# A four-layer graph network on one core: who makes the low halves in the first layer, the order of its stores and loads, and how early the first normalised tiles are made

## The reference

```python
h = jnp.maximum(_layernorm(x, axis=-1), 0.0)
x = x + _L0_gnn_ref(h, adj, L0_gnn_weightr, L0_gnn_weightd, L0_gnn_bias)
h = jnp.maximum(_layernorm(x, axis=-1), 0.0)
x = x + _L1_gnn_ref(h, adj, L1_gnn_W1, L1_gnn_W2)
h = jnp.maximum(_layernorm(x, axis=-1), 0.0)
x = x + _L2_gnn_ref(h, adj, L2_gnn_W, L2_gnn_b)
h = jnp.maximum(_layernorm(x, axis=-1), 0.0)
x = x + _L3_gnn_ref(h, adj, L3_gnn_W, L3_gnn_a, L3_gnn_wtrans)
return x
```

## Time and profile before

| | us |
|---|---|
| median of 3 runs (2110.57 to 2112.67) | 2111.86 |
| the profiled execution, own time | 2112.05 |
| its span in the trace | 2110.3 |
| PE busy | 2052.6 (97%) |
| DVE busy | 1326.5 (63%) |
| ACT busy | 1012.9 (48%) |
| POOL busy | 53.6 (3%) |

### The profile page before, as it was taken

The page is one execution under the profiler, slowest core; times in us unless marked ns, Lnnn a source line. Parts: engine busy times, 40 slices in busy tenths (PEclk is TensorE's granted clock), DMA queues, the critical chain, the costliest instruction groups (busy, mean ns, idle before and its releaser), DMA issues.

```text
span 2110.3 us, 26133 instructions
## 1 busy us (share of the span) xinstructions
PE 2052.6 (97%) x10560; PEld 1493.7 (71%) x10560; DVE 1326.5 (63%) x2040; ACT 1012.9 (48%) x1333; POOL 53.6 (3%) x88
## 2 busy tenths in 40 slices
PE   5999989999999999999999899999999999999998
PEld 4888865555545555554555588888888888888887
DVE  6855440000044242434548899999999999999674
ACT  6755440000020000001104679797888788787873
POOL 0011340000000000000000000000000000000000
PEclk9999999999999999999999999999999999999999
DMA  9997352010311223301157645444445444351200
GB/s 376 381 349 278 111 202 48 21 41 21 100 50 56 65 64 96 117 31 61 48 109 313 170 160 207 138 180 145 180 144 179 165 140 180 132 212 65 100 20 11
DMA packets 102393, 288.25 MB, mean 137 GB/s; under 512 B 45184, under 2 KB 52096, under 8 KB 85760
## 3 DMA queue, kind: packets, MB, share of 16 engines
q1 hardware_dynamic: 96896, 278.19, 38.3%
q10 hardware_dynamic: 5376, 8.39, 1.3%
HBM read 245.11 MB, written 33.06 MB: 132 GB/s over the span
## 4 chain that ended last, share of the span: by engine, by line
PE 90%; DVE 3%; DMA 2%; ACT 2%; POOL 1%; issue 1%; SPq 0%; ACTq 0%; POOLq 0%; DVEq 0%
PE ps L1822 41%; PE ps L1733 32%; PE ps L1593 7%; PE ps L1750 7%; PE ps L1792 2%; DMA h_spill<-work 1%; POOL work L649 1%; PE ps L1699 1%; DMA feat<-in_adj 1%; PE ps L1671 1%; PE ps L1660 1%; ACT big L686 0%; DMA big<-in_adj_t 0%; POOL work L664 0%; DVE feat L1426 0%
## 5 line engine op out<-in xcount | busy, mean ns | idle before, releaser
L1733 PE MATMUL ps<-big,feat 128*128 128x512 fp8e4 x3072 | 671.1, 381 | 11.3 <-DMA feat<-h_spill 7.1
L1733 PEld LDWEIGHTS ps<-big,feat 128*128 128x128 f16 x3072 | 301.4, 98 | 375.0 <-issue 12.9
L1822 PE MATMUL ps<-big,work 128*128 128x257 f32 x2048 | 450.9, 381 | 4.9 <-ACT work L961 4.9
L1822 PE MATMUL ps<-big 128*128 128x257 f32 x2048 | 449.4, 380 | 3.5 <-ACT big L961 3.5
L1822 PEld LDWEIGHTS ps<-big,work 128*128 128x128 f32 x2048 | 388.4, 190 | 60.8 <-issue 4.8
L1822 PEld LDWEIGHTS ps<-big 128*128 128x128 f32 x2048 | 388.3, 190 | 59.6 <-ACT big L961 4.4
L1593 PE MATMUL ps<-feat,big 128*128 128x256 f16 x2048 | 224.7, 273 | 0.0
L1593 PEld LDWEIGHTS ps<-feat,big 128*128 128x128 fp8e4 x2048 | 199.9, 98 | 23.4
L686 ACT ACTIVATE big<-big 128x2048 bf16<-128x2048 f32 (+1 forms) x124 | 182.3, 1487 | 13.2 <-DMA big<-in_adj_t 12.9
L953 ACT ACTIVATE big<-feat,uv_sb 128x512 f32<-128x512 f32 x256 | 163.3, 710 | 22.5 <-PE ps L1822 22.5
L953 ACT ACTIVATE work<-feat,uv_sb 128x512 f32<-128x512 f32 x256 | 163.4, 713 | 16.5 <-PE ps L1822 15.8
(11 more groups left out here) (165 smaller groups left out, 1365.9 us busy)
## 6 DMA issues: line engine op xcount, KB each, us to landing
big<-in_adj_t SPq DMA_DIRECT2D x64, 1024.0 KB, 4.9
feat<-in_adj SPq DMA_DIRECT2D x56, 1024.0 KB, 6.9
big<-in_adj_t SPq DMA_DIRECT2D x80, 512.0 KB, 9.6
h_spill<-work SPq DMA_DIRECT2D x31, 512.0 KB, 3.6
feat<-h_spill SPq DMA_DIRECT2D x31, 512.0 KB, 4.7
work<-in_adj_t SPq DMA_DIRECT2D x27, 512.0 KB, 6.7
x_spill<-work SPq DMA_DIRECT2D x24, 512.0 KB, 2.7
feat<-in_adj_t SPq DMA_DIRECT2D x21, 512.0 KB, 8.6
```

The costliest lines, as they stand in the source:

```text
L1733: ins = mm(ps[:, bank + f, :], parts[:, j, h, f * P:(f + 1) * P], adj_units[:, c, j, :], start=(fresh and h == 0), stop=(end and h == 1), ...
L1822: ins = mm(ps[:, 4 * s + t, 0:YW], quads[k % RING][:, jj, t * P:(t + 1) * P], Yb[:, j, s, :], start=(j == 0), stop=(j == NT - 1), skip_gro ...
```

## The change

`FIRST_TILE` goes from 2 to 0 and `STATS_AHEAD` from 4 to 3. `rows_of_a` and the copy of its result stand earlier. In the last stretch of layer 0 `low` leaves GpSimd for DVE, where it stands behind `bn_stats` of the same tile of the next chunk. SP issues `store_h(c - 1)` ahead of `refill(c)`. `low_done` is gone, and `post_done` counts layer 0 too.

```diff
-    FIRST_TILE = 2
-    STATS_AHEAD = 4
+    FIRST_TILE = 0
+    STATS_AHEAD = 3
...
                 def store_h(c):
                     s = c % 2
-                    if l == 0:
-                        sp.wait_ge(low_done, lows(c + 1))
-                    else:
-                        sp.wait_ge(post_done, (l - 1) * NC + c + 1)
+                    sp.wait_ge(post_done, l * NC + c + 1)
                     sp.dma_start(chunk_rows(hs, c), g_ring[:, s, :, :]).then_inc(h_out[s], 16)
...
                 if l == 0:
                     for c in range(NC - 1):
                         store_x(c)
+                        if c > 0:
+                            store_h(c - 1)
                         if c + 3 < NC:
                             refill(c, c % 2, c // 2)
-                        if c > 0:
-                            store_h(c - 1)
                     load_weights(1)
                     store_h(NC - 2)
...
-            def low(c, t):
-
-                n = c * TPC + t
-                pool.wait_ge(rect_ready, n + 1)
-                pool.wait_ge(hi_ready, n + 1)
-                both = h_ring[:, c % 2, t, :, :] if c < NC - 1 else parts[:, n, :, :]
-                nc.gpsimd.tensor_tensor(both[:, 1, :], rect_ring[:, t, :], both[:, 0, :], ALU.subtract)\
-                  .then_inc(low_done, 1)
-
             for c in range(NC):
                 for t in range(TPC):
                     residual(c, t)
-                    if 0 < c < NC - 1:
-                        low(c - 1, t)
-                if c == NC - 2:
-                    for t in range(TPC):
-                        low(c, t)
...
-                if n == 17:
+                if n == 14:
                     act.wait_ge(wa_ps_ready, 1)
...
                         if t == 0:
                             act.wait_ge(cols_ready, c + 1)
-                            wait(act, low_done, lows(c))
+                            wait(act, post_done, c)
...
                         if t == TPC - 1:
-                            ins.then_inc(low_done, 1)
+                            ins.then_inc(post_done, 1)
                         else:
                             ch.link(ins)
...
                             dve.wait_ge(residual_added, c * TPC + t + 1)
                             ch.link(nc.vector.bn_stats(stat[:, t, :], x_slots[c % 3][:, t, :]))
+                            if 0 < c < NC - 1:
+                                low(c - 1, t)
                         last_variance(ch.link)
...
-                        if c == NC - 1:
+                        if c >= NC - 2:
                             for t in range(TPC):
                                 low(c, t)
...
-                if q == 6:
+                if q == 5:
                     rows_of_a()
```

More of the change, by code:

```diff
@@ L211, in gnn_stack @@
                                                        sem("cols_ready"))
-        dsc0_ready, low_done = sem("dsc0_ready"), sem("low_done")
+        dsc0_ready = sem("dsc0_ready")
         small_in, weights_in = sem("small_in"), sem("weights_in")
@@ L347, in h_stores @@
             return 16 * (l * H + k - (1 if s == 1 and l > 0 else 0))
-        def lows(c):
-            return c * TPC if c < NC else (NC - 1) * TPC + 1
         def parts_needed(c, k):
@@ L480, in transpose_own @@
                     if l == 1 and c == NC - 1:
-                        sp.wait_ge(low_done, lows(NC))
+                        sp.wait_ge(post_done, NC)
                     elif l == 1:
@@ L792, in evac @@
                     if l == 1 and c == 0:
-                        act.wait_ge(low_done, lows(NC))
+                        act.wait_ge(post_done, NC)
                     act.wait_ge(group_done, c * GROUPS + (staged(l) + GROUPS))
@@ L1252, in _ @@
                     ch = Chain(0, 0)
-                    dve.wait_ge(post_done, NC)
+                    dve.wait_ge(post_done, 2 * NC)
                     ch.link(nc.vector.tensor_reduce(g_own, gmax[:, :], AX.X, ALU.max))
@@ L1726, in main @@
                             elif l == 1 and j == (NC - 1) * TPC:
-                                pe.wait_ge(low_done, lows(NC))
+                                pe.wait_ge(post_done, NC)
                             elif j % TPC == 0:
```

## The result

The changed kernel takes 2126.67 us (median of 4 runs, 2126.16 to 2130.84) against 2111.46 before (median of 4 as well, 2110.57 to 2112.67): 1.0075 times as long (95% interval 1.0062 to 1.0089), 15.2 us. The forecast was 2125.5. Its profiled execution took 2126.76 us with a span of 2125.0, 14.7 over that of before.

A forecast was written before the change was run, and what follows sets the result against it. PE (97% busy) was taken as the bound, standing still only before the long row and at the seam from layer 0 to 1. 2112.05 + 12.7 + 0.75 = 2125.5 us; own range 2120 to 2130, wider range 2114 to 2131.

The forecast's parts named there:

- Part one, the lead: First stretch: the means' lead of three steps shrinks to none, ACT and DVE wait in a loop; long row +12.7 us.
- The walk: First stretch followed step by step from piece 12: long row of products starts at 89.5 instead of 76.84 us.
- the clock term: First stretch: PE loses clock behind long gaps, product 2.99 instead of 1.89 us; +12.7 in all, +8.9 without loss.
- "shorter" gaps: First stretch: three PE gaps of about 1.5, 2.6 and 2.5 us; losing the clock there would cost 1.5 to 1.8 each.
- the bounds of 8.9 and 17: First stretch's delay: +8.9 us without any clock loss, +17 if the clock is also lost behind three shorter gaps.
- Part two, the store: Last stretch of layer 0: store ahead of load removes ACT's h_spill wait; six steps take 52 us instead of 61.9.
- Part three, low on DVE: Last stretch of layer 0: low collides with residual, step 10.5 us (9.25 without collision, 11.2 at most), spending the store's gain.
- the last stretch's term: Seam from layer 0 to 1: PE starts at 305.65, +0.75 us beside the first stretch's shift, idle still 7.8 us.
- The sum: Whole kernel: profiled execution 2112.05 + 12.7 (first stretch) + 0.75 (last stretch) = 2125.5 us.
- The collision does not bite: Rival, 17%: in the last stretch low is not held and the seam closes, -9.4 us there: 2115.4 us.
- The first stretch does nothing: Rival, 5%: DVE catches up in ACT's waits for pieces, low's collision bites: 2113 us, no difference.
- Worse clock: Rival, 15%: three shorter gaps in the first stretch lose the clock too, last-stretch step near 11: 2132 us.

The follow-up runs named there:

- experiment 1: The kernel before with only FIRST_TILE 0, STATS_AHEAD 3, and rows_of_a and its copy earlier: 2126.46 us, 1.0074 times before.
- experiment 5: The kernel before with STATS_AHEAD 1 alone, tiles left late (FIRST_TILE 2): 2121.33 us, 1.0045 times before.
- experiments 7 and 8: The kernel before with FIRST_TILE 0, STATS_AHEAD 6, rows_of_a and its copy earlier: 2115.31 us; the same with DVE's y0 copies back at their late places: 2112.00 us.
- experiment 2: The kernel before with store_h ahead of refill and nothing else, low left on GpSimd: 2103.76 us, 0.9965 times before.
- experiment 4: The changed kernel with the lows of chunks 0 to 6 replaced by a one-input tensor_reduce: 2119.84 us, 6.8 below the changed kernel.

## Why the prediction was right

**Part one, the lead.** The mechanism held: the first stretch alone makes the whole loss (experiment 1), and without the tiles' move the lost lead still makes 11.2 of the 16.3 us (experiment 5). The walk against the profile after:

| | predicted | measured |
|---|---|---|
| ACT's tile 12, behind the means of chunk 3 | 36.4 | 36.5 |
| tile 16 | 44.3 | 46.0 |
| first `degree_sums` | 45.5 | 47.2 |
| the product behind it done | 50.2 | 52.8 |
| tile 20 | 58.1 | 60.9 |
| tile 24 | 68.2 | 72.1 |
| tile 28 | 75.9 | 79.9 |
| second `degree_sums` | 84.8 | 88.6 |
| long row | 89.5 | 93.1 |

It is mis-sized by 3.6 us, all of it in the clock term; it arises up to tile 16 (1.6), in the product behind the first `degree_sums` (0.9) and up to tile 24 (1.1). The gap of 2.27 us ahead of 38.92, one of the three "shorter" gaps, did lose the clock (1.7 us); and behind the long gaps the first product took 3.62 us where I had put the 2.99 of the earlier trace rows, which had caught the clock's return halfway. 16.3 lies within the bounds of 8.9 and 17.

That the first row of the table fits to 0.1 us is luck. The walk began at piece 12, with a wait of DVE for a product behind a lost clock. In the trace PE kept its clock there (the product behind 30.36 took 1.89 us) and DVE did not wait at that place. It was late by as much because the loop had closed sooner: DVE had waited 3.82 us for a product, and ACT 3.18 us for the means of chunk 2, where the first such wait was forecast near 32 us:

```profile
21.66 0.69 DVE L1154 COPY feat<-ps 128x512 f32<-128x512 f32 x1 [3.82 <-PE ps L1652]
...
27.97 0.51 ACT L681 ACTIVATE work<-big,minus_mean 128x256 f32<-128x256 f32 x1 [3.18 <-DVE minus_mean L1147]
```

What the sum named only in passing is a cause of its own: the copy of q = 13 ahead of the second fold. With the lead restored, early tiles still cost 3.7 us at the row's start, and putting the copies back takes 2.8 of them away (experiments 7 and 8). The 0.9 left is within the scatter of that start, which in kernels with the first stretch of before lay between 76.84 and 78.98.

**Part two, the store.** As predicted: no wait for h_spill, and alone it closes the seam (experiment 2).

**Part three, low on DVE.** The step was put at 10.5 us and is 10.26, with 9.25 for a low that collides with nothing and 9.29 measured. The 0.24 too much lies in the three holds, put at 0.35 (`residual` 1), 0.57 (low 1) and 0.6 us (low 2), in the rows 0.28, 0.47 and 0.52. The 0.3 us that the lows of chunk 6 were to save did not come (10.69 us from that chunk's first tile to PE's start, put at 10.45). So the last stretch's term is -0.4 us (6.66 less 7.07) in place of +0.75; in this trace, for the same idle was 6.47 to 7.16 us in the six profiles whose last stretch is that of before. By the Trainium skill ("SBUF — State Buffer", "Who interferes with whom") a DVE instruction with two SBUF inputs contends with a GpSimd instruction that reads SBUF, and one with a single SBUF input does not. The two runs agree: with two inputs 0.90 and 0.95 us beside GpSimd, with one 0.42 in all 28.

**The sum.** +16.3 and -0.4 make 15.9 at the seam (320.83 less 304.89), but the spans differ by 14.7. The 1.2 us come off at the attention layer, which no edit touched: 0.5 ahead of its first products and 0.7 in them. There the profile of before has 3.5 us of PE waiting for ACT, that of the changed kernel 2.1 and the others 1.7 to 3.4: scatter between executions. The result came so close by luck, because the errors, +3.6, -1.15 and -1.2, went against each other.

**The rivals.** "The collision does not bite" fell to the two-input rows and experiment 4, which is that rival made real (2119.8 with the longer delay of the first stretch, against 2115.4). "The first stretch does nothing" fell to experiment 1. "Worse clock" was half true: one of its three gaps in this execution, and no step near 11.

## What to carry to other kernels

When two engines feed each other inside one in-order loop, a distance such as "statistics four tiles ahead" is not a tuning of memory but the slack of a ring: write down at which step each side makes what the other wants, and subtract. It can be too large by one at no price and turn into a wait at every round when it reaches none. An operation moved off an idle engine onto a busy one costs its length and its collisions; here one good line (the store ahead of the load, -7.4 us) was hidden behind two that cost, so try the lines of a change apart.

## What the runs showed of the hardware

An instruction of DVE that reads two SBUF tiles and one of GpSimd that reads SBUF hardly overlapped in the rows shown. Whichever came second, by as little as 0.01 us, ended 0.59 us (GpSimd, 0.73 alone) or 0.28 and 0.29 us (DVE, 0.43 alone) after the first, so at most 0.15 us of the two ran side by side. A tensor_reduce with one operand in the same place was held in none of 28 cases, nor was `linear` with one SBUF tile.

PE's clock stood at full speed behind gaps of 3.19 and 2.44 us in the changed kernel (the product behind the transposes of 30.36 took 1.89 us; from 88 to 94 us the granted clock was 1.00, the 2.4 GHz level), and was lost around gaps of 2.27, 3.68 and 4.48 us. In the kernel before it was lost behind one of 1.32 us. The same gap went both ways: in experiment 4, which has the first stretch of the changed kernel, the products behind the gap of 2.44 us ahead of the second `degree_sums` ran at 0.66. Ahead of the 2.27 and the 1.32 stood the small matmuls with two columns, but behind the same matmuls and a gap of 1.28 us experiment 4 kept it (1.00, the product 1.89 us). Neither the length of a gap nor these matmuls alone tell what it costs; what decides was not tested.
